# A Mamba scan loop: softplus' rounding term moves from VectorE to ScalarE and TensorE, one more C product moves from GpSimd to VectorE

## The reference

```python
u, x_gate = split(x @ in_proj_w)                    # 256 channels each
u = silu(depthwise_conv3(u) + conv_b)
delta, b, c = split(u @ x_proj_w)                   # 256, 16, 16
delta = softplus(delta @ dt_proj_w + dt_proj_b)
h_t = exp(delta_t * a) * h_(t-1) + delta_t * b_t * u_t     # a state of 16 per channel
y_t = sum_s h_t[s] * c_t[s]
out = ((y + u * D) * silu(x_gate)) @ out_proj_w
```

## Time and profile before

| what | value |
|---|---|
| median of 3 runs | 1401.25 us (1397.68 to 1401.56) |
| the profiled execution: its time | 1406.63 us |
| its span in the trace | 1404.9 us |
| mean granted TensorE clock | 0.889 of full |
| busy, share of the span: TensorE, VectorE, ScalarE, GpSimd | 78%, 79%, 63%, 67% |

### The profile page before, as it was taken

How to read it: one execution, slowest core, us unless ns; L and a number is a source line. 1 busy time by engine, 2 the same in 40 slices (tenths; PEclk the granted TensorE clock), 3 DMA queues, 4 the chain that set the end, 5 groups by cost and what they waited for, 6 DMA issues and landing times. The chain is left out here.

```text
span 1404.9 us, 15371 instructions
## 1 busy us (share of the span) xinstructions
PE 1099.2 (78%) x4128; PEld 508.5 (36%) x4128; DVE 1104.9 (79%) x1448; ACT 885.8 (63%) x1605; POOL 936.7 (67%) x501
## 2 busy tenths in 40 slices
PE   4767877787777877777778876437998989999796
PEld 2322222222222222222222221125655336666695
DVE  6499999999999999999999999885482962222288
ACT  3577577677677577667667665344333876666796
POOL 0199999999999999999999999721010740000176
PEclk9888899989999899989988898856899999999898
DMA  5645835835835835834834846100000001111013
GB/s 158 139 104 120 176 68 120 175 77 110 175 75 112 181 73 108 181 84 97 181 83 98 182 85 157 52 20 1 1 0 14 10 1 34 39 39 34 12 31 91
DMA packets 48490, 122.87 MB, mean 87 GB/s; under 512 B 5824, under 2 KB 20928, under 8 KB 42304
## 3 DMA queue, kind: packets, MB, share of 16 engines
q1 hardware_dynamic: 46864, 121.01, 38.9%
q10 hardware_dynamic: 1584, 1.36, 0.3%
HBM read 83.55 MB, written 5.24 MB: 63 GB/s over the span
## 5 line engine op out<-in xcount | busy, mean ns | idle before, releaser
L555 POOL TENSOR_TENSOR states<-b_dup,dup 128x1024 f32<-128x1024 f32 x256 | 597.0, 2363 | 65.7 <-DMA dup<-dd 64.0
L648 DVE TENSOR_TENSOR_SCAN da<-da,states 128x1024 f32<-128x1024 f32 x160 | 359.5, 2283 | 39.0 <-ACT da L397 33.0
L397 ACT ACTIVATE da<-dup,decay 128x510 f32<-128x510 f32 x512 | 327.2, 672 | 11.1 <-DVE states L648 11.1
L295 PE MATMUL yp<-states,fold 128*64 128x512 f32 x1024 | 275.8, 665 | 15.7 <-DVE states L574 9.8
L534 POOL TENSOR_TENSOR states<-states,X 128x1024 f32<-128x1024 f32 x96 | 226.6, 2360 | 20.8 <-DVE states L648 20.6
L648 DVE TENSOR_TENSOR_SCAN states<-da,states 128x1024 f32<-128x1024 f32 x96 | 218.7, 2278 | 7.0 <-ACT da L397 7.0
L574 DVE TENSOR_TENSOR states<-da,X 128x1024 f32<-128x1024 f32 x160 | 192.5, 1203 | 0.0
L1642 POOL TENSOR_SCALAR put<-row_t,slot_i,slot_w 128x256 f32<-128x256 f32 x32 | 39.1, 1222 | 193.5 <-POOLq L1346 173.5
L393 ACT ACTIVATE da<-zeros 128x4 f32<-128x4 f32 x177 | 30.6, 173 | 197.0 <-DVE states L574 196.3
L295 PEld LDWEIGHTS yp<-states,fold 128*64 128x64 f32 x1024 | 69.3, 152 | 213.0 <-issue 196.5
L1447 DVE TENSOR_TENSOR hx<-glx,upx 128x512 f32<-128x512 f32 x64 | 41.3, 684 | 126.6 <-ACT glx L1412 118.2
(11 more groups left out here) (183 smaller groups left out, 1766.0 us busy)
## 6 DMA issues: line engine op xcount, KB each, us to landing
b_dup<-bc_rows SPq DMA_DIRECT2D x32, 1024.0 KB, 9.5
dup<-dd SPq DMA_DIRECT2D x128, 256.0 KB, 11.7
X<-bc_rows SPq DMA_DIRECT2D x64, 512.0 KB, 11.5
out<-X SPq DMA_DIRECT2D x3, 1024.0 KB, 5.1
wg<-in_wgT SPq DMA_DIRECT2D x16, 128.0 KB, 2.1
wu<-in_wuT SPq DMA_DIRECT2D x16, 128.0 KB, 2.2
wd<-in_wdT SPq DMA_DIRECT2D x16, 128.0 KB, 2.2
bc_rows<-bcf SPq DMA_DIRECT2D x16, 64.0 KB, 1.6
```

The costliest lines, as they stand in the source:

```text
L295: last = nc.tensor.matmul(yp[64 * i:64 * i + 64, :], fold[:], states[:, (2 * step + i) % RING, s, :], start=False, stop=(q == 3 and s == S ...
L397: ins = nc.scalar.activation(factors[:, s, :].rearrange("p (b t) -> p b t", b=2)[:, :, 1:S], src[:, :, 1:S], ACT.Exp, scale=decay[:, col:c ...
L555: nc.gpsimd.tensor_tensor(states[:, i % RING], b_dup[:, par, s0:s0 + SPI, :], dup[:, par, 1, h, g, :].unsqueeze(1).broadcast_to([P, SPI, N ...
L648: nc.vector.tensor_tensor_scan(to.rearrange("p s t -> p (s t)"), factors.rearrange("p s t -> p (s t)"), ring.rearrange("p s t -> p (s t)") ...
```

## The change

`lost` is gone from VectorE. In its place ScalarE subtracts 1 from the PSUM buffer (an Identity with a bias of -1 from the new constant `minus`, signalled by `sp_less`), and TensorE adds -absx onto it as two further matmuls with `neg_ident`. `ON_POOL` loses item 11: its product with c is now made by VectorE out of PSUM. Since that item's result is now in buffer 1, the factors of item 14, its next user, wait for this product and write their first columns again. Ahead of the accumulations TensorE writes the two softplus buffers whole once (`whole_banks`): buffer 2 at its start, buffer 1 at the end of its prologue; ScalarE waits for both, for the second before the factors of item 0 of pair 0. The small product of the prologue's weights goes to `yp` instead of buffer 2.

```diff
-        ON_POOL = (1, 4, 6, 7, 11, 14)
+        ON_POOL = (1, 4, 6, 7, 14)
...
             def softplus(m):
 
-                pe.wait_ge(sp_lost, m + 1)
+                pe.wait_ge(sp_less, m + 1)
                 for h in range(H2):
+                    nc.tensor.matmul(soft(m)[:, h, :], neg_ident[:], absx[:, h, :], start=False, stop=False,
+                                     skip_group_check=True)
                     nc.tensor.matmul(soft(m)[:, h, :], neg_ident[:], logx[:, h, :], start=False, stop=False,
                                      skip_group_check=True)
...
+            def whole_banks(buffer):
+
+                for h in range(H2):
+                    last = nc.tensor.matmul(da[:, buffer, h, :], ident[:], ident[:].unsqueeze(1).broadcast_to([P, CH, P]),
+                                            start=True, stop=True)
+                last.then_inc(banks_whole, 1)
+
             pe.wait_ge(id_ready, 1)
+            whole_banks(SOFT_FIRST)
             turn(0)
...
             pe.wait_ge(tp_free, PAIRS)
+            whole_banks(SOFT)
...
             def log(m):
-                if not is_at(m, 0):
+                if is_at(m, 0):
+                    act.wait_ge(banks_whole, 1)
+                else:
                     free(m - 1, BEFORE_SOFT)
...
                 nc.scalar.activation(logx[:], soft(m), ACT.Ln).then_inc(sp_log, 1)
+                act.wait_ge(sp_log, m + 1)
+                nc.scalar.activation(soft(m), soft(m), ACT.Identity, bias=minus[:, 0:1]).then_inc(sp_less, 1)
...
             act.wait_ge(zeros_set, 1)
+            act.wait_ge(banks_whole, 2)
...
-            def lost(m):
-                dve.wait_ge(sp_log, m + 1)
-                nc.vector.scalar_tensor_tensor(soft(m), soft(m), -1.0, absx, ALU.add, ALU.subtract).then_inc(sp_lost, 1)
...
-                    if i == 6 and not last:
-                        lost(n + 1)
```

More of the change, by code:

```diff
@@ L96, in mamba @@
         zeros = sb("zeros", [P, 2 * SPI, 1])
+        minus = sb("minus", [P, 1])
         skip_diag = sb("skip_diag", [P, H2, P])
@@ L125, in mamba @@
         tp = da[:, 0:2].rearrange("p k s n -> p (k s) n")
-        wp = da[:, 2]
+        wp = yp[:].rearrange("p (c n) -> p c n", c=2)
         QT, QP = TILES // 4, PAIRS // 4
@@ L165, in mamba @@
         sp_log = sem("sp_log")
-        sp_lost = sem("sp_lost")
+        sp_less = sem("sp_less")
         sp_sum = sem("sp_sum")
         zeros_set = sem("zeros_set")
+        minus_set = sem("minus_set")
+        banks_whole = sem("banks_whole")
         delta_ready = sem("delta_ready")
@@ L329, in _ @@
                 for r in range(2):
-                    last = nc.tensor.matmul(wp[:, c, 0:DI], w_xdT[:, r, c * P:(c + 1) * P], w_dt[:, r, :],
+                    last = nc.tensor.matmul(wp[:, c, :], w_xdT[:, r, c * P:(c + 1) * P], w_dt[:, r, :],
                                             start=(r == 0), stop=(r == 1))
@@ L466, in _ @@
             act.wait_ge(wp_ready, 1)
-            nc.scalar.activation(w_delta[:], wp[:, :, 0:DI], ACT.Copy).then_inc(wd_ready, 1)
+            nc.scalar.activation(w_delta[:], wp, ACT.Copy).then_inc(wd_ready, 1)
             nc.scalar.preload_act_table_set(LOG_EXP)
@@ L472, in _ @@
             negative_exp(0, before(DELTA1))
+            act.wait_ge(minus_set, 1)
             log(0)
@@ L542, in _ @@
             nc.gpsimd.memset(xhT[:, :, SP1 - 1:SP1], 0.0).then_inc(pads_ready, 1)
+            nc.gpsimd.memset(minus[:], -1.0).then_inc(minus_set, 1)
             nc.gpsimd.memset(zeros[:], 0.0).then_inc(zeros_set, 1)
@@ L637, in _ @@
             norm(1)
-            lost(0)
             inputs(0, 0)
```

## The result

The changed kernel takes 1408.47 us (median of 6 runs, 1407.62 to 1409.40); the kernel before, run beside it, took 1399.47. The ratio is 1.0048, its 95% interval 1.0028 to 1.0069: slower, by 9.0 us between the medians (the interval is 3.9 to 9.7 us). The forecast was 1406.5 and slower.

A forecast was written before the change was run, and what follows sets the result against it. The loop was taken as VectorE's work plus its waits for ScalarE, GpSimd following. Loop waits -17.9, products +17.9, `lost` 0, prologue +5.3: 1401.25 + 5.3 = 1406.5 us, range 1403 to 1414.

The forecast's parts named there:

- `lost` worth 0: Item 7 in the loop: removing `lost` from VectorE saves 0 in 15 pairs; its time becomes waiting for ScalarE's factors.
- That rival (1389.5): Removing `lost` pays: item 7's scan moves up 1.14 us in 15 pairs, -17.1 us; chance 0.06.
- The subtraction free: ScalarE behind the softplus logarithm: the 1.1 us subtraction fits in 2.10 us of idle time, cost 0.
- The longer sum at the upper level: TensorE's softplus sum with two more matmuls takes 5.4 us at 2.4 GHz; item 10 waits 0.33 us in each pair.
- The rival at the lower level (1438): TensorE stays at 1.2 GHz through the softplus sum: item 10 waits 2.44 us, 31.7 us more in all; chance 0.08.
- Product of item 11, +17.9: VectorE in the loop: 16 products of item 11 at 1.12 us each add 17.9 us.
- wait (a): VectorE's wait at item 2, behind ScalarE's SiLU and table loads: falls to 0.48 us in 14 pairs, 6.7 us.
- the bound of 20.31: Longest distance in us from the gate after item 11 to item 2's scan, with TensorE slow; 19.90 was taken.
- GpSimd's relief 0: Loop: GpSimd gives up 16 x 2.31 us, worth 0 because nobody waits for it.
- The rival in which GpSimd is the bound (1373): GpSimd sets the loop's pace: VectorE's 34.4 us of waits go, giving 5.3 - 33.6 us; chance 0.06.
- Prologue +5.3: Prologue: ScalarE waits for buffer 1's filling, so item 2's scan comes 6.05 us later, 0.71 regained; bounds 3.6 to 9.
- The rival that it is made up in pair 0: The prologue's delay is made up in pair 0: no change, 1400 to 1404 us; chance 0.18.

The follow-up runs named there:

- refilled slot: The changed kernel with a VectorE sum that nobody reads where `lost` stood, in 15 pairs: 1407.58 us.
- three matmuls: The kernel before with three useless zero-weight matmuls behind each second gate projection, in TensorE's idle stretch, and nothing else: 1383.41 us.
- The softplus change alone: The changed kernel with item 11's product back on GpSimd (six products there): 1406.99 us, ratio 1.0050 to the kernel before.
- the product alone: The kernel before with item 11's product on VectorE and nothing else: 1409.07 us, ratio 1.0058.
- the earlier fill: The changed kernel with the second bank filling between the two convolutions of pair 1 instead of behind both: 1405.39 us.
- the softplus change with the useless matmuls: The changed kernel with item 11 back on GpSimd, the earlier fill, and three useless matmuls behind each second gate projection: 1385.22 us.

## Why the prediction was right

The direction and the mechanism were right; one term was mis-sized, and one hit its number in part by luck. The time came nearer (1406.5 to 1408.47) than the difference (5.3 to 9.0), because the kernel before had 1401.25 us when it was forecast from and 1399.47 beside the changed kernel.

- **`lost` worth 0: right.** Item 7 waits 1.46 us in each pair, and the refilled slot left the time as it was. That rival (1389.5) is out.
- **The subtraction free: right.** 1.09 us, 0.98 of cover left.
- **The longer sum at the upper level: right.** 5.42 us for 5.4 forecast; item 10 at 0.33 in all pairs. The rival at the lower level (1438) is out.
- **Product of item 11, +17.9, wait (a) down to 6.7: the size was off.** (a) came to 9.8. The step took 19.90 us from gate to scan in every pair; in five of fourteen it was longer, up to 20.86 (gate at 479.07, scan at 499.93) and so over the bound of 20.31, as TensorE stayed longest at its lower level behind its gate. The bound for all pairs together (+5.7) still holds the +3.1 of the loop. What the step did not see is how much of (a) that level was making already: it named SiLU and table loads, and TensorE's lateness only with 0.41 us, but 14 of the 19.9 us went with three matmuls. The softplus change alone shows what that omission can cost: its gain at item 10 came back as a wait at item 2.
- **GpSimd's relief 0: right.** Its waits grew by 43 us (37 forecast), VectorE never waited for it, and the product alone cost 6.4 us. The rival in which GpSimd is the bound (1373) is out. The Trainium skill, Perfetto Trace Analysis, "Identifying the Most-Contended Engine", would relieve the busiest engine; at 97% GpSimd was that, and the trace disagrees, since VectorE never waited for it in the loop.
- **Prologue +5.3: the mechanism right, the number in part luck.** 5.4 by the trace shown, with ScalarE's wait for the fill at its root; the earlier fill gave 3.1 to 3.6 of it back. But two other executions with the same prologue cost it 1.0, under the bound of 3.6: the step took TensorE's earlier matmuls as it found them, and there they ran faster. The rival that it is made up in pair 0 is out: only the 0.71 was.

The 8.5 us of the trace and the 9.0 of the medians agree within what single executions differ by: from the last gate to the end, the expert layer, it took 497.5 us in the profiled execution of before and 492.7 in that of the changed kernel.

## What to carry to other kernels

When two engines look equally full, read the waits before the shares: work taken from the engine that nobody waits for only becomes its waiting time. Before pricing a wait by the engine that it names, look at the engine behind that one and at the pace of its instructions there: a matmul at half pace right behind an idle stretch suggests that part of the wait is the clock's, and useless matmuls are a cheap test. A gain at one item of a loop should be followed through the whole pair, because the same cause can take it back at another.

## What the runs showed of the hardware

TensorE's level at one place decided more than the whole change: three useless matmuls of 2.74 us in each of the 15 pairs, which cut an idle stretch of 3.48 to 4.40 us to 1.18 or 1.73, took 19 us off a kernel in whose loop VectorE never waits for TensorE itself, only for ScalarE. The granted clock over 91 to 850 us rose from 0.89 to 0.95 there, and from 0.91 to 0.96 in the changed kernel. And the fall can come after work has begun again: in the pair at 317.94 above, the skip matmul took 1.24 us and the sum behind it 3.47 instead of 1.94.

The length of the idle stretch alone does not say what follows. In the kernel before, the five pairs in which item 2 waits longest (2.00 to 2.06 us) have the shortest stretches, 3.48 to 3.59 us; what goes with the wait is how long the lower level lasts, for there the sum takes 3.47 to 3.53 us and elsewhere 2.45 to 2.90. Behind the same 3.25 us the softplus sum takes 5.12 to 5.40 us in nine pairs and 6.61 to 6.68 in five. And after only 1.73 us the sum behind the skip matmul still fell to 3.47 us in one pair of the softplus change with the useless matmuls, at 669.24.
